# First attention of a two-layer kernel: each batch's normalisation, transpose and projection moved one period ahead, and its normalisation moved from VectorE to ScalarE

## The chip, the cores and the metric

The kernel runs on one core of one Trainium2 chip. The metric is the device time of one execution in microseconds (us). The engines are TensorE (PE, with its weight loads as PEld), VectorE (DVE), ScalarE (ACT), GpSimd (POOL) and SyncE (SP), which here only issues DMAs. Each engine works through its own list of instructions in order; they meet at semaphores alone.

## The reference, cut to what matters

The program computes two transformer layers. The change touches only the first attention of the first layer, whose input `x` has 16 batches of 256 tokens with 128 channels:

```python
h = _ln(x, ln1_g, ln1_b)                  # (x - mean) * rsqrt(var + 1e-5) * g + b
q, k, v = jnp.split(h @ w_qkv + b_qkv, 3, axis=-1)      # 16 heads of 8 channels
# buckets of 64 tokens; a bucket sees the one before it and, causally, itself
scores = where(mask, einsum('bnihd,bnjhd->bnhij', qb, kc) * scale, -inf)
ob = einsum('bnhij,bnjhd->bnihd', softmax(scores), vc)
x = x + ob @ w_out + b_out
h2 = _ln(x, ln2_g, ln2_b)                 # goes into the MLP and the first expert layer
```

What follows it (the dense MLP and eight dense experts, a second attention, a routed expert layer) is not changed.

## The kernel before, in words

`attention_0` runs from the start to 274 us of the span. It is a software pipeline over 16 batches, one batch (256 tokens, two tiles of 128 rows) entering in each period. Its order is written out by hand in `PARTS_0` (line 173): a period `s` has four parts, each a list of steps `(name, stage, k)`, and a step with stage `g` works in period `s` on batch `s - g`. `parts_0` (line 188) hands the same sequence to all engines, and each engine does what it has to do for a step (`step` under `block.gpsimd`, `scalar`, `vector`, `tensor`). So the place of a step in the list sets its place in four queues at once. "s3" below is the period with s = 3.

The front of a batch has these steps:

- `xstats`: VectorE takes mean and variance of two token tiles (lines 505 and 509).
- `power`: GpSimd turns variances into reciprocal roots (lines 369 and 370), in one pair of instructions for the first norm of batch `s` and the second norm of batch `s - 5`.
- `norm`: VectorE writes `hn = (x - mean) * rstd` (lines 525 and 527); GpSimd, in the same place, computes `shift2` (lines 390 and 392) for the second norm, and adds the output bias to `x` (line 403).
- `lift`: TensorE transposes `hn` (line 602) and, for the batch four behind, the attention output `ob` (line 606); ScalarE copies both out of PSUM as `hT` (line 429) and `aT` (line 431).
- `qk`: TensorE projects `hT` to keys and queries in fp32 (lines 610 and 611); ScalarE writes their fp16 high part (line 438), `low` on VectorE the rest (line 534). SyncE writes both to DRAM and reads them back in head order into one of three `kq` tiles (lines 337, 339 and 346), which the scores of the next period read.
- `vproj`: TensorE and VectorE make the values (lines 618 and 541).

In the period in which batch n has its scores (s = n + 2), part k has `scores` (PE lines 635 and 641, DVE row maxima line 547), `mpad` and `shift` (the maxima subtracted from the queries, line 562); `weights` one period later (PE line 657, ACT exp line 446, POOL causal mask line 411), `values` (PE line 670), `copy` and `back` (ACT line 451, PE line 679, DVE lines 570 and 571), `output` (PE line 693, DVE lines 580 and 582), `stats` (line 515), `norm2` (ACT line 457), PE transposes of `hn2` inside `output` (line 691), `halves2` (ACT lines 466 and 469, POOL line 395). `split` (ACT lines 474 and 476) and `wlow` (POOL line 398) prepare the dense weights of the next stage alongside.

Before, the front is split over the turn of a period: batch s has `xstats` in part 0, `power` in part 2 and `norm` in part 3 of period s; its `lift`, `qk` and `low` follow in part 0 of period s + 1, in front of the `weights` of that part. PSUM bank `WA` holds the transposes first and then the projection, so one batch's `lift` waits for the last `low`. Scores use two banks `S`, weights two banks `ST`.

SyncE also issues, behind the read-back of each batch, up to five DMAs that fill DRAM rows with a constant (`blanks`, line 356, 268 KB each, 72 in all), after batch 0 the rest of `x` and the dense constants and weights (lines 349, 2416 and 2423), and later further dense weights.

Of the kernel before, what the change touches and what calls it, by code (L numbers as in the profile page):

```python
# [9 lines left out]
P = 128  # L10
# [8 lines left out]
NC_ = T // CT  # L19
# [137 lines left out]
def unpacked(m, name):  # L157
# [4 lines left out]
    for part, shape in parts:  # L162
# [8 lines left out]


PARTS_0 = [
    [("scores", 2, 0), ("lift", 1, 0), ("vproj", 2, 0), ("shift", 3, 1), ("qk", 1, 0), ("xstats", 0, 0), ("low", 1, 0),
     ("weights", 3, 0), ("values", 4, 3), ("copy", 4, 1)],
    [("scores", 2, 1), ("mpad", 2, 0), ("output", 5, 0), ("back", 4, 1),
     ("weights", 3, 1), ("values", 3, 0), ("halves2", 6, 0), ("wlow", 0, 0)],
    [("scores", 2, 2), ("shift", 2, 0), ("stats", 0, 0),
     ("weights", 3, 2), ("power", 0, 0), ("values", 3, 1), ("copy", 3, 0)],
    [("scores", 2, 3), ("mpad", 2, 1), ("back", 3, 0), ("norm", 0, 0),  # L180
     ("weights", 3, 3), ("values", 3, 2), ("norm2", 5, 0), ("split", 0, 0)]]
STAGES_0 = 6
ONE_HIGH, ONE_LOW = 3, 19
AHEAD = NB - 2
# [3 lines left out]
def parts_0(step):  # L188

    for s in range(NB + STAGES_0 - 1):  # L190
        for part in PARTS_0:
            for what, stage, k in part:
                if what == "lift":
                    if s > 0:
                        step(what, s - 1, k)
                elif what in ("xstats", "stats", "power", "norm"):
                    if s < AHEAD + 5:
                        step(what, s, k)
                elif what in ("halves2", "norm2"):
                    if 0 <= s - stage < AHEAD:  # L200
                        step(what, s - stage, k)
                elif what == "split":
                    if 0 <= s - 2 < CUTS:
                        step(what, s - 2, k)
                elif what == "wlow":
                    if 0 <= s - 3 < CUTS:
                        step(what, s - 3, k)
                elif 0 <= s - stage < NB:
                    step(what, s - stage, k)


def attention_0(nc, d, keep, rows, heads, stages):
# [3 lines left out]
    with ExitStack() as ctx:  # L216
# [12 lines left out]
        mv = m.sb("mv", [P, 4, 2])  # L229
        half = m.sb("half", [P, 4])  # L230
        rstd = m.sb("rstd", [P, 4])
        shift2 = m.sb("shift2", [P, 2])
        hn2 = m.sb("hn2", [P, 2, C])
        h2 = m.sb("h2", [P, TB])
# [30 lines left out]
        xb_done = m.sem("xb_done")  # L265
        ln = m.sem("ln")
        var_done = m.sem("var_done")
        rstd_done = m.sem("rstd_done")
        pool_ln = m.sem("pool_ln")
        passed_pool, passed_dve = m.sem("passed_pool"), m.sem("passed_dve")  # L270
        hn_done = m.sem("hn_done")
        lift_full, lift_free = m.sem("lift_full"), m.sem("lift_free")
# [17 lines left out]
        x1_done = m.sem("x1_done")  # L290
        shift2_done, norm2_done = m.sem("shift2_done"), m.sem("norm2_done")
        h2_done, xh_done, xl_done = m.sem("h2_done"), m.sem("xh_done"), m.sem("xl_done")
        shift2_own = m.sem("shift2_own")
# [8 lines left out]
        def both_norms(n):  # L302
            return slice(0 if n < NB else 2, 4 if n >= 5 else 2)

        def toks2(n):
            return slice(n * TB, (n + 1) * TB)
# [13 lines left out]
        def _(sp):  # L320
# [6 lines left out]
                sp.wait_ge(kq_clear, p + 1)  # L327
                sp.dma_start(kq[p][ONE_HIGH:P:16, 0], d["unit"]).then_inc(ones_in, 16)
            sp.wait_ge(loaded, 16 * LOADS)
            sp.dma_start(x[:, 4:12, :], d["x"][:, 4:12, :]).then_inc(x_mid, 16)  # L330
            sp.dma_start(keep["gate0"][:], d["gate0"]).then_inc(gate_in, 16)
            for n in range(NB):
                planes = heads[n % 2]
                sp.wait_ge(high_done, n + 1)
                wait(sp, landed[n % 2], 48 * (n // 2))
                for i in (1, 3):
                    sp.dma_start(planes[i:i + 2].rearrange("s p t -> p s t"), high[:]).then_inc(high_out, 16)
                sp.wait_ge(low_done, n + 1)
                sp.dma_start(planes[0:6:5].rearrange("s p t -> p s t"), low[:]).then_inc(low_out, 16)

                sp.wait_ge(high_out, 32 * (n + 1))
                wait(sp, st_full, n * 8 - 16)
                for c, pair in enumerate((planes[2:4], planes[0:2], planes[4:6])):
                    if c == 1:
                        sp.wait_ge(low_out, 16 * (n + 1))
                    sp.dma_start(kq[n % 3][c:P:4, :, :, BK:BK + TB].rearrange("r s a t -> r (s a) t"),
                                 pair.rearrange("s (a r) t -> r (s a) t", a=4)).then_inc(landed[n % 2], 16)
                if n == 0:
                    sp.dma_start(x[:, 12:NT, :], d["x"][:, 12:NT, :]).then_inc(x_rest, 16)
                    keep["fetch_dense"](sp)  # L350
                    sp.wait_ge(blank_set, 1)
                if n % 2 == 0 and n >= 4:
                    sp.wait_ge(w_low, n - 2)
                    keep["fetch_set"](sp, n // 2)
                for i in range(5 * n, min(5 * n + 5, BLANKS * NC_)):
                    sp.dma_start(blanks[:, i], blank[:]).then_inc(blanked, 16)
            sp.wait_ge(w_low, 2 * E - 2)
            keep["fetch_set"](sp, E)
# [3 lines left out]
        def _(pool):  # L362
            def power(n):
                pool.wait_ge(var_done, n + 1)

                wait(pool, norm2_done, n - 5)
                settle(pool, passed_pool)
                t, v = Tally(pool, pool_ln, 1, n), both_norms(n)
                t.link(pool.tensor_scalar(rstd[:, v], mv[:, v, 1], EPS, 1.0, ALU.add, ALU.mult))
                pool.tensor_tensor(rstd[:, v], rstd[:, v], half[:, v], ALU.pow).then_inc(rstd_done, 1)  # L370

            pool.memset(half[:], -0.5).then_inc(half_set, 1)
            pool.wait_ge(half_set, 1)
# [8 lines left out]
            pool.wait_ge(loaded, 16 * LOADS)  # L382

            def step(what, n, k):
                if what == "power" and n:
                    power(n)
                if what == "norm" and n >= 5:

                    pool.wait_ge(rstd_done, n + 1)
# [6 lines left out]
                if what == "wlow":  # L396
                    pool.wait_ge(w_high, n + 1)
                    pool.tensor_tensor(cut_of(("w1l", "w2l"), n), stage[:, n // 2 % 2, n % 2],
                                       cut_of(("w1h", "w2h"), n), ALU.subtract).then_inc(w_low, 1)
                if what == "norm" and n < NB:  # L400
                    rows_landed(pool, n)
                    for a in range(2):
                        ins = pool.tensor_tensor(keep["xs"][:, 2 * n + a, :], x[:, 2 * n + a, :], bo[:], ALU.add)
                    ins.then_inc(xb_done, 1)
# [13 lines left out]
        def _(act):  # L418
# [6 lines left out]
            def step(what, n, k):  # L425
# [21 lines left out]
                if what == "copy":  # L447
                    act.wait_ge(pv_done, n * 8 + 4 * k + 4)

                    wait(act, back_full, n * 2 - 1 + k)  # L450
                    act.activation(ots[:, k, :], OT[:], ACT.Copy).then_inc(ot_free, 1)
                if what == "norm2":
                    act.wait_ge(shift2_done, n + 1)

# [28 lines left out]
        def _(dve):  # L483
            dve.memset(mpad[:], 0.0).then_inc(cleared, 1)
            for t in hT:
                dve.memset(t[:, 0:BK], 0.0).then_inc(cleared, 1)
            for t in kq[0:2]:
                dve.memset(t[:], 0.0).then_inc(kq_clear, 1)
            sums = Tally(dve, ln, 0, 0)

            def step(what, n, k):
# [9 lines left out]
                if what == "xstats" and n < NB:  # L501
                    wait(dve, rstd_done, n)
# [4 lines left out]
                    settle(dve, passed_dve)  # L507
                    for a in range(2):
                        ins = dve.bn_aggr(mv[:, a, :], st[:, a, :])
                        ins.then_inc(var_done, 1) if a and n < 5 else sums.inc(ins)  # L510
                if what == "stats" and n >= 5:
                    wait(dve, rstd_done, n)
# [4 lines left out]
                    settle(dve, passed_dve)  # L517
                    for a in range(2):
                        ins = dve.bn_aggr(mv[:, 2 + a, :], st[:, 2 + a, :])
                        ins.then_inc(var_done, 1) if a else sums.inc(ins)  # L520
                if what == "norm" and n < NB:

                    wait(dve, lift_full, n)
                    dve.wait_ge(rstd_done, n + 1)
                    dve.tensor_scalar(hn[:, 0, :], x[:, 2 * n, :], mv[:, 0, 0:1], rstd[:, 0:1],
                                      ALU.subtract, ALU.mult)
                    dve.tensor_scalar(hn[:, 1, :], x[:, 2 * n + 1, :], mv[:, 1, 0:1], rstd[:, 1:2],
                                      ALU.subtract, ALU.mult).then_inc(hn_done, 1)
                    if n == 0:
                        dve.memset(kq[2][:], 0.0).then_inc(kq_clear, 1)  # L530
# [2042 lines left out]
```

## Time and profile before

| | us |
|---|---|
| median of 3 runs | 1055.04 (1055.03 to 1056.13) |
| the profiled execution | 1056.1 |
| its span | 1054.3 |
| first attention within the span | 0 to 274 |
| PE busy over the span | 917.5 (87%) |
| DVE busy | 822.5 (78%) |
| ACT busy | 748.9 (71%) |
| POOL busy | 431.6 (41%) |

The span runs from the first to the last recorded instruction. Times of single rows are microseconds from its start. A row of the timeline gives start, duration, engine, line, operation, tiles, and how many like instructions it merges; in brackets stands the idle time of that engine just ahead of it and what ended it.

### The profile page before, as it was taken

To read this page: it belongs to the slowest core of one execution; us is meant where nothing else is said; L and a number is where in the kernel's file an instruction comes from. 1 tells how busy PE (TensorE), PEld (TensorE's weight loads), DVE (VectorE), ACT (ScalarE), POOL (GpSimd) and SP (SyncE) were. 2 spreads that over 40 slices of the span, in tenths; PEclk is the share of its full clock that TensorE was granted. 3 is DMA by queue.
4 is the path that set the end of the run, shared out by engine and by line. 5 is a ranking of instruction groups with operands and counts; after the bars stand their busy time and mean duration, and the time that the engine had idled before them with its cause. 6 is when DMAs were issued, how large, how long until landed. Compare 5 with 4: busy or idle time off the path is not lost. (4 is left out here: it accounts for less than half of the span.)

```text
span 1054.3 us, 28529 instructions
## 1 busy us (share of the span) xinstructions
PE 917.5 (87%) x9966; PEld 576.0 (55%) x9966; DVE 822.5 (78%) x2280; ACT 748.9 (71%) x1482; POOL 431.6 (41%) x613
## 2 busy tenths in 40 slices
PE   3688888887799999999999999869888865899995
PEld 2466656665355444444444444446556544788862
DVE  4587787875477799868899989958888867888854
ACT  1256666666799888888888878547677644688854
POOL 4255666667245200000000011014588877676653
PEclk9598999999799999999999999979999985999999
DMA  6635555541100000032122222111111102233318
GB/s 192 211 116 173 174 185 165 164 139 33 32 1 1 2 1 1 1 95 80 67 73 80 83 60 79 32 34 51 32 46 51 58 27 76 73 86 85 83 48 217
DMA packets 85578, 84.50 MB, mean 80 GB/s; under 512 B 8978, under 2 KB 62484, under 8 KB 85440
## 3 DMA queue, kind: packets, MB, share of 16 engines
q1 hardware_dynamic: 76240, 71.49, 22.0%
q0 software_dynamic: 4544, 8.60, 2.5%
q10 hardware_dynamic: 4656, 2.59, 0.9%
q8 instruction: 84, 1.38, 0.5%
q14 instruction: 54, 0.44, 0.1%
HBM read 45.77 MB, written 37.78 MB: 79 GB/s over the span
## 5 line engine op out<-in xcount | busy, mean ns | idle before, releaser
L931 ACT ACTIVATE d__hf<-keep__banks,dense__d 128x512 f32<-128x512 f32 x288 | 185.5, 680 | 48.2 <-PE keep__banks L1169 47.2
L995 DVE TENSOR_TENSOR d__hl<-d__hf,d__hh 128x1024 f16<-128x1024 f32 x144 | 174.1, 1220 | 28.0 <-ACT d__hh L936 25.8
L936 ACT ACTIVATE d__hh<-d__hf 128x1024 f16<-128x1024 f32 x144 | 152.2, 1057 | 4.6
L915 POOL TENSOR_SCALAR d__rstd<-d__mv 128x4 f32<-128x4 f32 x16 | 13.9, 869 | 336.7 <-DVE d__mv L1123 336.7
L411 POOL TENSOR_SCALAR_AFFINE_SELECT a__pt<-a__pt 128x512 f32<-128x512 f32 x128 | 81.5, 660 | 93.6 <-ACT a__pt L446 93.6
L1167 PE MATMUL keep__banks<-dense__xh,dense__w1h 128*128 128x512 f16 x288 | 109.9, 382 | 2.9 <-ACT d__hf L931 1.7
L1167 PE MATMUL keep__banks<-d__hh,dense__w2h 128*128 128x512 f16 x288 | 109.2, 379 | 2.4 <-DVE d__tmp L1052 2.4
L1169 PE MATMUL keep__banks<-dense__xh,dense__w1l 128*128 128x512 f16 x288 | 109.9, 381 | 0.0
L1168 PE MATMUL keep__banks<-dense__xl,dense__w1h 128*128 128x512 f16 x288 | 109.9, 381 | 0.0
L1168 PE MATMUL keep__banks<-d__hl,dense__w2h 128*128 128x512 f16 x288 | 109.2, 379 | 0.0
L1169 PE MATMUL keep__banks<-d__hh,dense__w2l 128*128 128x512 f16 x288 | 109.2, 379 | 0.0
L446 ACT ACTIVATE a__pt<-keep__banks 128x512 f32<-128x512 f32 x128 | 69.4, 596 | 43.7 <-PE keep__banks L657 43.6
L547 DVE TENSOR_REDUCE a__mx<-keep__banks 128x4 f32<-128x512 f32 x128 | 81.8, 682 | 20.4 <-PE keep__banks L641 20.2
L1458 POOL DMA_INDIRECT parts<-c__ys,c__dest x78 | 81.2, 1041 | 39.7 <-issue 16.6
L1897 POOL DMA_INDIRECT rows<-b__xr,b__slot x64 | 63.6, 994 | 21.5 <-issue 17.0
L1476 ACT ACTIVATE c__hf<-keep__banks,c__bias 128x256 f32<-128x256 f32 x156 | 61.1, 474 | 7.5 <-PE keep__banks L1685 6.4
L1697 PE MATMUL keep__banks<-routed__w2h,c__hh 128*128 x312 | 55.8, 219 | 5.4 <-DVE c__hl L1612 5.4
L1612 DVE TENSOR_TENSOR c__hl<-c__hf,c__hh 128x512 f16<-128x512 f32 x78 | 54.2, 695 | 2.7
L1699 PE MATMUL keep__banks<-routed__w2h,c__hl 128*128 x312 | 55.5, 219 | 0.0
L1698 PE MATMUL keep__banks<-routed__w2l,c__hh 128*128 x312 | 55.5, 219 | 0.0
L635 PE MATMUL keep__banks<-a__kq 32*64 32x128 f16 x1024 | 31.8, 229 | 20.7 <-DMA a__kq<-heads 18.3
L1167 PEld LDWEIGHTS keep__banks<-dense__xh,dense__w1h 128*128 128x128 f16 x288 | 30.4, 105 | 35.4 <-ACT d__hf L931 3.2
(353 smaller groups left out, 2330.8 us busy)
## 6 DMA issues: line engine op xcount, KB each, us to landing
rows<-a__blank SPq DMA_DIRECT2D x72, 268.0 KB, 3.8
d__G<-gates SPq DMA_DIRECT2D x64, 256.0 KB, 3.1
a__kq<-heads SPq DMA_DIRECT2D x48, 128.0 KB, 2.9
c__xin<-rows SPq DMA_DIRECT2D x39, 134.0 KB, 2.3
heads<-a__high SPq DMA_DIRECT2D x32, 128.0 KB, 2.2
dense__stage<-e_w SPq DMA_DIRECT2D x16, 256.0 KB, 3.6
b__stage<-e_w SPq DMA_DIRECT2D x32, 128.0 KB, 2.3
heads<-a__low SPq DMA_DIRECT2D x16, 128.0 KB, 2.0
```

Of the source, the lines that this page charges most:

```text
L411: pool.affine_select(out=v, in_=v, compare_op=ALU.is_ge, fill=0.0, base=BK, pattern=[[0, 8], [1, BK]], channel_multiplier=-1).then_inc(cau ...
L446: act.activation(pt[:, u % 4, :], ST[:, u % 2, :], ACT.Exp, scale=scale).then_inc(exp_done, 1)
L547: dve.tensor_reduce(mx[:, u // 4, :, u % 4], S[:, u % 2, :].rearrange("p (a j) -> p a j", a=4), AX.X, ALU.max).then_inc(s_free, 1)
L931: act.activation(hf[:, q, f], HB[:, f], gelu, scale=1.0 / WS, bias=b1[:, at:at + 1]).then_inc(s_["h_free"], 1)
L936: act.activation(hh[:, j % (LEAD + 1), f - 1:f + 1], hf[:, q, f - 1:f + 1], ACT.Copy).then_inc(s_["hi_done"], 1)
L995: dve.tensor_tensor(hl[:, p, f], hf[:, q, f], hh[:, p, f], ALU.subtract).then_inc(s_["lo%d_done" % i], 1)
L1167: pe.matmul(dst, wh, vh, start=begin, stop=False)
L1168: pe.matmul(dst, wh, vl, start=False, stop=False)
L1169: return pe.matmul(dst, wl, vh, start=False, stop=end)
L1458: pool.indirect_dma_start(parts, bass.IndirectOffsetOnAxis(dest[b % RING][:, a:a + 1], 0), ys[b % RING][:, a, :], None, bounds_check=2 * T ...
L1476: ins = act.activation(hf[b % 2][:, f], HB[:, b % 2, f // 2, f % 2], ACT.Gelu, scale=1.0 / WS, bias=bias[:, f, b:b + 1])
L1897: pool.indirect_dma_start(rows, bass.IndirectOffsetOnAxis(slot[n % SENT][:, k, a:a + 1], 0), words[n % SENT][:, a, :], None, bounds_check= ...
```

## The change

The steps of the front are regrouped. In period s, batch s now has `xstats` and a new `xpower` in part 0, a new step `hnorm` at the end of part 1, `lift` in part 2, `qk` and `low` in part 3. `hnorm` is two ScalarE activations (`Identity` with scale `rstd` and bias `shift`) in place of VectorE's two `tensor_scalar`. GpSimd computes that bias `shift = -mean * rstd` in `xpower`, so the power of the first norm and that of the second (`power2`) are now separate pairs. `norm2` moves from the end of part 3 to the front of the next part 0. `lift` of the attention output moves with `lift`. SyncE issues the second piece of `x` after batch 0 instead of ahead of it, the third piece, the dense data and the blanks after batch 1.

```diff
 PARTS_0 = [
-    [("scores", 2, 0), ("lift", 1, 0), ("vproj", 2, 0), ("shift", 3, 1), ("qk", 1, 0), ("xstats", 0, 0), ("low", 1, 0),
-     ("weights", 3, 0), ("values", 4, 3), ("copy", 4, 1)],
+    [("scores", 2, 0), ("norm2", 6, 0), ("vproj", 2, 0), ("shift", 3, 1), ("xstats", 0, 0),
+     ("weights", 3, 0), ("xpower", 0, 0), ("values", 4, 3), ("copy", 4, 1)],
     [("scores", 2, 1), ("mpad", 2, 0), ("output", 5, 0), ("back", 4, 1),
-     ("weights", 3, 1), ("values", 3, 0), ("halves2", 6, 0), ("wlow", 0, 0)],
-    [("scores", 2, 2), ("shift", 2, 0), ("stats", 0, 0),
+     ("weights", 3, 1), ("values", 3, 0), ("halves2", 6, 0), ("hnorm", 0, 0), ("wlow", 0, 0)],
+    [("norm", 0, 0), ("scores", 2, 2), ("lift", 0, 0), ("shift", 2, 0), ("stats", 0, 0),
      ("weights", 3, 2), ("power", 0, 0), ("values", 3, 1), ("copy", 3, 0)],
-    [("scores", 2, 3), ("mpad", 2, 1), ("back", 3, 0), ("norm", 0, 0),
-     ("weights", 3, 3), ("values", 3, 2), ("norm2", 5, 0), ("split", 0, 0)]]
+    [("scores", 2, 3), ("mpad", 2, 1), ("qk", 0, 0), ("back", 3, 0), ("low", 0, 0), ("sums", 0, 0),
+     ("weights", 3, 3), ("values", 3, 2), ("split", 0, 0)]]
@@ SyncE @@
             sp.wait_ge(loaded, 16 * LOADS)
-            sp.dma_start(x[:, 4:12, :], d["x"][:, 4:12, :]).then_inc(x_mid, 16)
-            sp.dma_start(keep["gate0"][:], d["gate0"]).then_inc(gate_in, 16)
             for n in range(NB):
...
                 if n == 0:
+                    sp.dma_start(x[:, 4:12, :], d["x"][:, 4:12, :]).then_inc(x_mid, 16)
+                    continue
+                if n == 1:
                     sp.dma_start(x[:, 12:NT, :], d["x"][:, 12:NT, :]).then_inc(x_rest, 16)
                     keep["fetch_dense"](sp)
+                    sp.dma_start(keep["gate0"][:], d["gate0"]).then_inc(gate_in, 16)
                     sp.wait_ge(blank_set, 1)
...
-                for i in range(5 * n, min(5 * n + 5, BLANKS * NC_)):
+                for i in range(5 * n - 5, min(5 * n, BLANKS * NC_)):
@@ GpSimd @@
             def power(n):
                 pool.wait_ge(var_done, n + 1)
-
-                wait(pool, norm2_done, n - 5)
+                wait(pool, hn_done, n)
                 settle(pool, passed_pool)
-                t, v = Tally(pool, pool_ln, 1, n), both_norms(n)
-                t.link(pool.tensor_scalar(rstd[:, v], mv[:, v, 1], EPS, 1.0, ALU.add, ALU.mult))
-                pool.tensor_tensor(rstd[:, v], rstd[:, v], half[:, v], ALU.pow).then_inc(rstd_done, 1)
+                t = Tally(pool, pool_ln, 1, n)
+                t.link(pool.tensor_scalar(rstd[:, 0:2], mv[:, 0:2, 1], EPS, 1.0, ALU.add, ALU.mult))
+                pool.tensor_tensor(rstd[:, 0:2], rstd[:, 0:2], half[:, 0:2], ALU.pow).then_inc(rstd_done, 1)
+                pool.tensor_scalar(shift[:], mv[:, 0:2, 0], -1.0, 1.0, ALU.mult, ALU.mult).then_inc(shift_own, 1)
+                pool.wait_ge(rstd_done, n + 1)
+                pool.wait_ge(shift_own, n + 1)
+                pool.tensor_tensor(shift[:], shift[:], rstd[:, 0:2], ALU.mult).then_inc(shift_done, 1)
+
+            def power2(n):
+                pool.wait_ge(var2_done, n + 1)
+
+                wait(pool, norm2_done, n)
+                settle(pool, passed_pool)
+                t = Tally(pool, pool_ln2, 1, n)
+                t.link(pool.tensor_scalar(rstd[:, 2:4], mv[:, 2:4, 1], EPS, 1.0, ALU.add, ALU.mult))
+                pool.tensor_tensor(rstd[:, 2:4], rstd[:, 2:4], half[:, 2:4], ALU.pow).then_inc(rstd2_done, 1)
@@ ScalarE @@
+                if what == "hnorm":
+
+                    wait(act, lift_full, n)
+                    act.wait_ge(shift_done, n + 1)
+                    for a in range(2):
+                        ins = act.activation(hn[:, a, :], x[:, 2 * n + a, :], ACT.Identity, scale=rstd[:, a:a + 1],
+                                             bias=shift[:, a:a + 1])
+                    ins.then_inc(hn_done, 1)
@@ VectorE @@
-                if what == "norm" and n < NB:
-
-                    wait(dve, lift_full, n)
-                    dve.wait_ge(rstd_done, n + 1)
-                    dve.tensor_scalar(hn[:, 0, :], x[:, 2 * n, :], mv[:, 0, 0:1], rstd[:, 0:1],
-                                      ALU.subtract, ALU.mult)
-                    dve.tensor_scalar(hn[:, 1, :], x[:, 2 * n + 1, :], mv[:, 1, 0:1], rstd[:, 1:2],
-                                      ALU.subtract, ALU.mult).then_inc(hn_done, 1)
...
```

The GpSimd step `sums` in part 3 keeps what `norm` did there (`shift2`, and the bias added to `x`); the wait of `xstats` on the last `rstd` becomes one on the last `shift`.

## Rows read from the trace of the kernel before

**Rows 1.** Timeline of PE: the scores that open s2, s3, s8, s16 and s17, and the first row of s18.
```profile
18.21 0.67 PE L635 MATMUL keep__banks<-a__kq 32*64 32x128 f16 x16 [7.24 <-DMA a__kq<-heads]
...
36.57 0.67 PE L635 MATMUL keep__banks<-a__kq 32*64 32x128 f16 x16 [7.34 <-DMA a__kq<-heads]
...
110.44 0.45 PE L635 MATMUL keep__banks<-a__kq 32*64 32x128 f16 x16 [0.62 <-DMA a__kq<-heads]
...
225.52 0.45 PE L635 MATMUL keep__banks<-a__kq 32*64 32x128 f16 x16
...
240.54 0.45 PE L635 MATMUL keep__banks<-a__kq 32*64 32x128 f16 x16 [0.50 <-DMA a__kq<-heads]
...
251.59 0.44 PE L606 MATMUL keep__banks<-keep__ident,a__ob 128*128 128x128 f32 x2
```

**Rows 2.** Busy time in period s11: length, PE, PEld, DVE, ACT, POOL, clock, DMA share, GB/s.
```profile
153.18:167.63 14.45, 12.06 (x311) 9.03 (x310) 11.47 (x33) 9.67 (x21) 9.27 (x17) 1.00 0.51 155
```

**Rows 3.** Timeline of PE in s11, from its lift on.
```profile
154.92 0.41 PE L602 MATMUL keep__banks<-keep__ident,a__hn 128*128 128x128 f32 x2 [0.97 <-DVE a__hn L527]
...
156.28 0.39 PE L647 MATMUL keep__banks<-a__a,a__mpad 128*128 128x128 f16 x4
157.50 0.70 PE L610 MATMUL keep__banks<-a__hT,a__a 128*128 128x256 f32 x2 [0.83 <-ACT a__aT L431]
...
158.57 0.41 PE L657 MATMUL keep__banks<-a__q,a__kq 32*128 32x64 f16 x16
...
159.49 0.45 PE L635 MATMUL keep__banks<-a__kq 32*64 32x128 f16 x16
...
160.09 0.38 PE L691 MATMUL keep__banks<-keep__ident,a__hn 128*128 128x128 f32 x2
...
161.02 0.66 PE L679 MATMUL keep__banks<-keep__ident,a__ots 128*128 128x128 f32 x4
161.61 0.40 PE L657 MATMUL keep__banks<-a__q,a__kq 32*128 32x64 f16 x16
...
163.51 0.38 PE L647 MATMUL keep__banks<-a__a,a__mpad 128*128 128x128 f16 x4 [0.21 <-DVE a__ob L571]
...
164.75 0.55 PE L635 MATMUL keep__banks<-a__kq 32*64 32x128 f16 x16
...
165.90 0.66 PE L679 MATMUL keep__banks<-keep__ident,a__ots 128*128 128x128 f32 x4 [0.27 <-ACT a__ots L451]
...
167.55 0.45 PE L635 MATMUL keep__banks<-a__kq 32*64 32x128 f16 x16
```

**Rows 4.** Timeline of DVE in s11: the normalisation of a batch.
```profile
154.18 0.34 DVE L525 TENSOR_SCALAR a__hn<-a__x,a__mv,a__rstd 128x128 f32<-128x128 f32 x1 [0.69 <-POOL a__rstd L370]
154.44 0.34 DVE L527 TENSOR_SCALAR a__hn<-a__x,a__mv,a__rstd 128x128 f32<-128x128 f32 x1
```

**Rows 5.** Timeline of POOL ahead of that normalisation.
```profile
151.42 1.27 POOL L411 TENSOR_SCALAR_AFFINE_SELECT a__pt<-a__pt 128x512 f32<-128x512 f32 x2
...
153.05 1.02 POOL L370 TENSOR_TENSOR a__rstd<-a__rstd,a__half 128x4 f32<-128x4 f32 x1
...
154.43 0.20 POOL L392 TENSOR_TENSOR a__shift<-a__shift,a__rstd 128x2 f32<-128x2 f32 x1
```

**Rows 6.** Timeline of ACT in s11.
```profile
154.66 0.88 ACT L457 ACTIVATE a__hn<-keep__lease,a__shift,a__rstd 128x128 f32<-128x128 f32 x2 [1.10 <-POOL a__shift L392]
...
162.05 1.08 ACT L446 ACTIVATE a__pt<-keep__banks 128x512 f32<-128x512 f32 x2 [1.08 <-PE keep__banks L657]
...
163.62 0.42 ACT L469 ACTIVATE dense__xh<-a__h 128x256 f16<-128x256 f32 x1
```

**Rows 7.** Timeline of SP: the writes of batches 0, 1 and 10, that start their round trips.
```profile
11.88 0.89 SPq L337 DMA_DIRECT2D heads<-a__high  x2
...
25.79 1.55 SPq L337 DMA_DIRECT2D heads<-a__high  x2
...
159.53 0.89 SPq L337 DMA_DIRECT2D heads<-a__high  x2
```

More of the change, by code:

```diff
@@ L193, in parts_0 @@
                 if what == "lift":
-                    if s > 0:
-                        step(what, s - 1, k)
-                elif what in ("xstats", "stats", "power", "norm"):
+                    if s < NB + 4:
+                        step(what, s, k)
+                elif what in ("stats", "power", "sums"):
                     if s < AHEAD + 5:
@@ L231, in attention_0 @@
         rstd = m.sb("rstd", [P, 4])
+        shift = m.sb("shift", [P, 2])
         shift2 = m.sb("shift2", [P, 2])
@@ L267, in attention_0 @@
         var_done = m.sem("var_done")
-        rstd_done = m.sem("rstd_done")
-        pool_ln = m.sem("pool_ln")
+        var2_done = m.sem("var2_done")
+        rstd_done, rstd2_done = m.sem("rstd_done"), m.sem("rstd2_done")
+        pool_ln, pool_ln2 = m.sem("pool_ln"), m.sem("pool_ln2")
         passed_pool, passed_dve = m.sem("passed_pool"), m.sem("passed_dve")
@@ L292, in attention_0 @@
         h2_done, xh_done, xl_done = m.sem("h2_done"), m.sem("xh_done"), m.sem("xl_done")
+        shift_own, shift_done = m.sem("shift_own"), m.sem("shift_done")
         shift2_own = m.sem("shift2_own")
@@ L300, in cut_of @@
             return keep[names[a]][:, e * CT:(e + 1) * CT]
-        def both_norms(n):
-            return slice(0 if n < NB else 2, 4 if n >= 5 else 2)
         def toks2(n):
@@ L384, in step @@
             def step(what, n, k):
-                if what == "power" and n:
+                if what == "xpower" and n:
                     power(n)
-                if what == "norm" and n >= 5:
-                    pool.wait_ge(rstd_done, n + 1)
+                if what == "power" and n >= 5:
+                    power2(n - 5)
+                if what == "sums" and n >= 5:
+                    pool.wait_ge(rstd2_done, n - 4)
                     pool.tensor_scalar(shift2[:], mv[:, 2:4, 0], -1.0, 1.0, ALU.mult, ALU.mult).then_inc(shift2_own, 1)
@@ L399, in step @@
                                        cut_of(("w1h", "w2h"), n), ALU.subtract).then_inc(w_low, 1)
-                if what == "norm" and n < NB:
+                if what == "sums" and n < NB:
                     rows_landed(pool, n)
@@ L486, in _ @@
                 dve.memset(t[:, 0:BK], 0.0).then_inc(cleared, 1)
-            for t in kq[0:2]:
-                dve.memset(t[:], 0.0).then_inc(kq_clear, 1)
+            dve.memset(kq[0][:], 0.0).then_inc(kq_clear, 1)
+            dve.memset(kq[1][:], 0.0).then_inc(kq_clear, 1)
             sums = Tally(dve, ln, 0, 0)
@@ L500, in step @@
                     dve.wait_ge(cleared, CLEARS)
-                if what == "xstats" and n < NB:
-                    wait(dve, rstd_done, n)
+                if what == "xstats":
+                    wait(dve, shift_done, n)
                     rows_landed(dve, n)
@@ L509, in step @@
                         ins = dve.bn_aggr(mv[:, a, :], st[:, a, :])
-                        ins.then_inc(var_done, 1) if a and n < 5 else sums.inc(ins)
+                        ins.then_inc(var_done, 1) if a else sums.inc(ins)
                 if what == "stats" and n >= 5:
-                    wait(dve, rstd_done, n)
                     wait(dve, shift2_done, n - 5)
@@ L519, in step @@
                         ins = dve.bn_aggr(mv[:, 2 + a, :], st[:, 2 + a, :])
-                        ins.then_inc(var_done, 1) if a else sums.inc(ins)
-                if what == "norm" and n < NB:
-                    wait(dve, lift_full, n)
-                    dve.wait_ge(rstd_done, n + 1)
-                    dve.tensor_scalar(hn[:, 0, :], x[:, 2 * n, :], mv[:, 0, 0:1], rstd[:, 0:1],
-                                      ALU.subtract, ALU.mult)
-                    dve.tensor_scalar(hn[:, 1, :], x[:, 2 * n + 1, :], mv[:, 1, 0:1], rstd[:, 1:2],
-                                      ALU.subtract, ALU.mult).then_inc(hn_done, 1)
-                    if n == 0:
-                        dve.memset(kq[2][:], 0.0).then_inc(kq_clear, 1)
+                        ins.then_inc(var2_done, 1) if a else sums.inc(ins)
+                if what == "norm" and n == 0:
+                    dve.memset(kq[2][:], 0.0).then_inc(kq_clear, 1)
                 if what == "low":
```

## The prediction

> **What bounds the kernel now.** I read the timeline of TensorE first, for the scores that open each period. The reader is to see three stretches [rows 1]: a start with two long waits for the read-back of keys and queries (7.24 and 7.34 us), a steady run from s8 to s16 of (225.52 - 110.44) / 8 = 14.39 us a period, and an end. Then the busy times in one steady period [rows 2]: of 14.45 us TensorE is busy 12.06, VectorE 11.47, ScalarE 9.67, GpSimd 9.27. No engine fills it, so a chain across engines sets it. The timelines name its members. TensorE waits 0.97 us ahead of the lift for VectorE's `hn` and 0.83 ahead of the projection for ScalarE's copy `aT` [rows 3]. VectorE's normalisation had itself waited 0.69 us for GpSimd's power [rows 4], which came behind a causal mask (1.27 us) in GpSimd's queue and took 1.02 us for four columns [rows 5]. The front of a batch is handed from engine to engine without work laid between the steps.
>
> **The change, part by part.** I walk one new steady period from lift to lift; where a step follows its forerunner directly I take the distance between starts in the old trace.
> - Part 2: the lift is followed by shift, weights, values and the scores of part 3. Lift and `vproj` together were 156.28 - 154.92 = 1.36 us; both stay on the path. Shift, weights and values to the next scores: 164.75 - 163.51 = 1.24.
> - Part 3: scores 160.09 - 159.49 = 0.60; projection 158.57 - 157.50 = 1.07; back transposes, weights, values to the next scores 167.55 - 165.90 = 1.65.
> - Part 0: scores 0.60, shift 0.39, then weights, values, the scores of part 1 and the output product 161.02 - 158.57 = 2.45.
> - Part 1: back transposes to the weights 161.61 - 161.02 = 0.59 [all rows 3]. From there the path leaves TensorE: weights, exps and `halves2` on ScalarE end at 163.62 + 0.42 = 164.04 [rows 6], 2.43 us after 161.61. Behind them stands the new `hnorm`, two activations of the kind of `norm2`: 0.88 us [rows 6]. To the lift 0.14, as from VectorE's end at 154.78 to 154.92 [rows 3, 4].
>
> Sum: 1.36 + 1.24 + 0.60 + 1.07 + 1.65 + 0.60 + 0.39 + 2.45 + 0.59 + 2.43 + 0.88 + 0.14 = 13.40 us, a gain of 1.0 per period. On TensorE itself the stretch from those weights to the lift is only about 0.34 + 0.58 + 0.60 = 1.5 us (weights, values, scores), so TensorE would still stand 3.45 - 1.5 = 1.9 us ahead of the lift. Both old waits go; this one is late next.
>
> Work that I cost at nothing, and its cover. GpSimd: one more power pair and one more shift pair; the pair on two columns in place of four is shorter, so I put the addition at 1.1 us, 10.4 in all, below the period. `xpower` follows the mask of part 0 and would give `shift` some 1 us ahead of `hnorm`; if that cover is gone, the lift is later by the excess, one for one. ScalarE: 0.88 more, 10.55 us. `norm2` now stands ahead of the exps of part 0; it fits while `split` ends 0.8 us before these weights do, and if not, the copy that the back transposes of part 1 need is late: by my walk it ends 0.1 to 0.2 us before TensorE comes to them, the thinnest cover of all. VectorE: 0.60 us less [rows 4], and no wait for power, since `xstats`, `stats` and `low` all read what was made parts ago. `low` waits for `high`, but the back step lies between, and scores and row maxima of the next part start together. SyncE: the same DMAs. Its new gate is the same wait on the weights of three batches before, which now end in the very part in which the write starts; they end first by a little. Queued behind it are read-back and blanks only.
>
> VectorE did a batch's normalisation in 0.60 us [rows 4], ScalarE needs 0.88 for the same shape [rows 6], and that stands on the path of every period. The Trainium skill, "ScalarE: Activation LUTs", section "Rules for kernel authors", speaks against it: multiplications and additions belong on VectorE. The rows agree as to the durations; by the rule the same order with VectorE normalising would gain 0.28 us more a period, some 3 us in all, if VectorE had it ready as early. What the rule leaves out is the place in the queue, worth the other 1.0.
>
> The **start**. Batch 0's front is longer by 0.28 us for ScalarE and some 0.4 for the two shift instructions, so its round trip starts at about 12.6 in place of 11.88 [rows 7]. Batch 1's front now waits for `low` of batch 0 (13.5), then takes statistics 0.9, `xpower` 1.5, `hnorm` 0.9, transposes and copy 1.3, projection 2.2 and high part 0.85, estimates at the durations of the first rows: write at about 21.3. Before, it was issued at 25.79 [rows 7], behind dense data and five blanks in SyncE's queue, and landed at 36.57 [rows 1]: 10.8 us, where batch 0's took 18.21 - 11.88 = 6.3. With those DMAs moved behind batch 1, I take 6.3: landed at 27.6. Then not the DMA but the work of s2 is last: it starts behind the projection of batch 1 at 20.1 and holds some 11.5 us, so s3 opens at 31.6 in place of 36.57: -5.0. The bounds are 36.57 + 0.7 (congestion as before) and 27.6.
> s3 to s7: 110.44 - 36.57 = 73.87 before. TensorE stood at its lower level in part of it (16 score matmuls took 0.67 us, later 0.45 [rows 1]). I take five periods of 13.5: -6.4. s8 to s15: 8 x 13.40 = 107.2 against 115.1: -7.9.
> s16: no front is left in it, since the last projection is now in s15. It took 240.54 - 225.52 = 15.0 and would take what s17 did without lift of `hn` and projection, 251.59 - 240.54 = 11.05: -4.0 [rows 1]. s17 and the end: nothing; the last value, back, lift and output steps are the same chain.
>
> Sum: -5.0 - 6.4 - 7.9 - 4.0 = -23.3, so 1056.1 - 23.3 = 1032.8 for the profiled execution. That execution was 1.1 us above the median, which makes 1031.7; some of the starts I used hold old waits (the 1.65 and 2.45 above), so I round down: **1031**.
>
> **The rivals.**
> 1. *The wait at the lift vanishes.* ScalarE's work up to `hnorm` comes earlier than I think, or TensorE is slower around it. Then VectorE is the bound: 11.47 - 0.60 busy and some 0.7 of hand-overs, 11.6 us a period. Eleven periods at 1.8 less: about 1011. For it: 11.47 is near. Against it: exps, `halves2` and `hnorm` have to follow the weights in ScalarE's queue, whatever TensorE does.
> 2. *ScalarE or GpSimd slips.* The copy in part 0 behind `norm2` and `split`, or the mask behind `xpower` and `power2`, makes TensorE wait as well: with 0.8 us more, 14.2 a period, eleven times, 1040. For it: both queues grow, to 10.5 us, and the cover is 0.2 us. Against it: each has 3 us of idle time in a period.
> 3. *Slower: the round trip becomes the bound.* The write of a batch starts 0.65 us before the next period and must be back one period later, so 13.4 + 0.65 = 14.05 us are there. A trip took 167.55 - 159.53 = 8.0 us or less in s11 [rows 3, 7], 10.8 behind blanks. It costs time above 14.05. To make the kernel slower it must also eat the gain elsewhere: at 17.5 us each of thirteen periods is 16.85, 3.4 more than mine, +44 in all, 1075; it breaks even near 15.9. Against it: blanks now follow a read-back by a whole period less its own length.
> 4. *No change.* Saved waits come back at one place per period, as `hn` late by 1.9 + 1.0 us and the start as congested as before: 1055.
>
> **How the numbers follow.** Forecast 0.64, rival 1 0.11, rival 2 0.17, rival 3 0.04, rival 4 0.04. The forecast's own range is 1024 to 1038: the start at its two bounds is -4 or +5, and the period uncertain by 0.3. With rival 2 whole, and reaching a third of the way to rival 1 for periods that fall between, the range is 1018 to 1044; left out are rivals 1, 3 and 4, 0.19. About 0.2%, 2 us, is what a measurement of this kernel can tell from no change. Faster by more: 0.64 + 0.11 + 0.17 = 0.92, and a little of rival 4; within it 0.04; slower 0.04.
>
> **What would show it.** In the changed trace: periods of 13.2 to 13.6 us between the opening scores from s7 to s16; TensorE idle 1.5 to 2 us ahead of the lift, ended by ScalarE's `hn`; no wait ahead of the projection; s3 opening near 31.6 and batch 1's write near 21.3; s16 of about 11. A period under 12, with no wait for `hn`, is rival 1. Waits of the back transposes for `ots`, or of values for the mask, with `hn` later than 2 us, are rival 2. Opening scores that wait for the read-back in steady periods are rival 3.

## The result, and the profile after

The changed kernel takes 1045.03 us (median of 6 runs, 1041.16 to 1047.99) against 1055.03 before (6 runs): ratio 0.9912, 95% interval 0.9883 to 0.9941. It is faster, by 10 us where 24 were forecast, and it stands outside the range of 1018 to 1044.

The page of the changed kernel. Its profiled execution took 1046.9 us:
```profile
span 1045.2 us, 28598 instructions
...
PE 925.2 (89%) x9966; PEld 588.5 (56%) x9966; DVE 810.5 (78%) x2248; ACT 761.4 (73%) x1514; POOL 445.1 (43%) x667
...
PEclk9698888988999999999999999969999965999998
```
VectorE lost 12 us of work, ScalarE and GpSimd gained 12.5 and 13.5, as planned. TensorE gained 7.7 us, though no matmul was added. The slices of PEclk are 26 us wide; the fourth to the tenth read 8 in all but one, where before they read 9 in all but one.

TensorE's timeline of the changed kernel, one row per question of the forecast (columns as in [rows 1]):
```profile
32.11 0.67 PE L650 MATMUL keep__banks<-a__kq 32*64 32x128 f16 x16
...
39.12 0.41 PE L672 MATMUL keep__banks<-a__q,a__kq 32*128 32x64 f16 x16 [3.16 <-ACT a__pt L462]
...
110.89 0.41 PE L617 MATMUL keep__banks<-keep__ident,a__hn 128*128 128x128 f32 x2 [1.65 <-ACT a__hn L473]
...
126.39 0.41 PE L617 MATMUL keep__banks<-keep__ident,a__hn 128*128 128x128 f32 x2 [1.65 <-ACT a__hn L473]
...
139.04 0.66 PE L617 MATMUL keep__banks<-keep__ident,a__hn 128*128 128x128 f32 x2 [1.65 <-ACT a__hn L473]
```
s3 opens at 32.11 (36.57 in [rows 1]). The two waits of [rows 3] are one now, 1.65 us ahead of the lift, and it is the same each time. The projection no longer waits. But the distances between lifts are not the same: 15.50 and 12.65 us here.

Windows from lift to lift (length; busy us and instructions of PE, PEld, DVE, ACT, POOL; granted clock; DMA share; GB/s), four periods in a row and then all of s8 to s15:
```profile
96.79:110.89 14.10, 12.45 (x303) 10.04 (x303) 10.97 (x31) 10.24 (x22) 10.26 (x21) 0.88 0.50 169
110.89:126.39 15.50, 13.85 (x303) 11.06 (x303) 10.95 (x31) 10.59 (x22) 10.29 (x21) 0.78 0.45 144
126.39:139.04 12.65, 11.01 (x302) 8.96 (x303) 10.71 (x31) 10.24 (x22) 10.28 (x21) 0.99 0.70 239
139.04:154.58 15.54, 13.89 (x302) 11.07 (x303) 11.10 (x32) 10.49 (x22) 10.36 (x21) 0.79 0.42 124
...
102.90:218.11 115.21, 101.44 (x2423) 81.34 (x2417) 87.32 (x249) 83.22 (x177) 82.32 (x160) 0.87 0.52 171
```
Every period holds the same some 303 matmuls, and the same busy time of VectorE, ScalarE and GpSimd. What differs is TensorE's clock. At a granted clock of 0.99 the period is 12.65 us, shorter than the forecast of 13.40; at 0.88 it is 14.10, at 0.78 it is 15.50. In each of the four, TensorE's busy time and the 1.65 us add up to the period: it waits at the lift and nowhere else. Before, the clock was 1.00 in a steady period [rows 2].

Three windows of one microsecond around one lift show where it falls:
```profile
137.04:138.04 1.00, 0.36 (x5) 0.08 (x2) 0.94 (x4) 0.97 (x4) 1.00 (x3) 1.00 0.95 327
138.04:139.04 1.00, 0.00 (x0) 0.03 (x1) 1.00 (x2) 0.86 (x3) 1.00 (x2) 0.84 0.97 356
139.04:140.04 1.00, 0.99 (x6) 0.94 (x7) 0.14 (x1) 0.00 (x0) 1.00 (x2) 0.50 0.99 354
```
TensorE runs nothing from 137.39 to 139.04 (the last row ahead of the lift starts at 137.00 and takes 0.39 us). Within that wait the granted clock drops from 1.00 to 0.50, and the work of the next period starts at 1.2 GHz in place of 2.4. That is why the lift's row at 139.04 holds two transposes in 0.66 us instead of 0.41. Most falls come a little later, with TensorE already at work again, which is why the lift at 110.89 still took 0.41. Behind the lift at 82.63, windows from it on:
```profile
82.63:83.63 1.00, 1.00 (x24) 0.88 (x24) 0.11 (x1) 0.34 (x1) 1.00 (x2) 1.00 0.98 347
83.63:84.63 1.00, 1.00 (x54) 0.78 (x49) 0.85 (x5) 1.00 (x4) 0.27 (x1) 0.74 1.02 367
84.63:85.63 1.00, 1.00 (x19) 0.77 (x17) 0.21 (x3) 0.96 (x2) 0.84 (x2) 0.50 0.37 133
```
Ten lifts, from 82.63 to 210.49 us, wait 1.65 us. The clock fell at seven of them and not at the other three (126.39, 184.22 and 197.25).

The gain and the loss, in us of the span:

| stretch | before | after | change | forecast |
|---|---|---|---|---|
| start to s3 | 36.57 | 32.11 | -4.5 | -5.0 |
| s3 to s7 | 73.87 | 70.79 | -3.1 | -6.4 |
| s8 to s15 | 115.08 | 115.21 | +0.1 | -7.9 |
| s16 | 15.02 | 11.32 | -3.7 | -4.0 |
| s17 to the first dense matmul | 33.31 | 32.11 | -1.2 | 0 |
| the rest, unchanged code | 780.45 | 783.66 | +3.2 | 0 |

Eight steady periods, the core of the change, brought nothing.

### The profile page after: what moved, and what is told of

Same layout as the page of the kernel before. It is cut to its first block and busy times, and to the rows that moved or that the text cites. A ratio compares the mean times of both kernels' runs of the same rounds, so it can differ in the third digit from the quotient of the medians.

```text
span 1045.2 us, 28598 instructions
## 1 busy us (share of the span) xinstructions
PE 925.2 (89%) x9966; PEld 588.5 (56%) x9966; DVE 810.5 (78%) x2248; ACT 761.4 (73%) x1514; POOL 445.1 (43%) x667
## 5 line engine op out<-in xcount | busy, mean ns | idle before, releaser
L685 PE MATMUL keep__banks<-a__pt,a__va 128*32 128x64 f32 x2048 | 48.6, 238 | 3.2 <-POOL a__pt L427 2.3
```

## The experiments

Two theories stood at the start. **A, the clock:** the chain got shorter as forecast, but the waits of TensorE are now one long one per period, in which its clock falls; the lost time is TensorE working at half speed after it. **B, the chain:** the added work of ScalarE or GpSimd stretches some periods (the second rival of the forecast), and TensorE's clock falls because it has to wait. Diffs are against the changed kernel unless it says otherwise. A ratio is to the kernel before as it ran beside that variant on the same chip, with its 95% interval in brackets; the variants ran on three chips, where the kernel before had medians of 1053.2 to 1054.4 us, so a difference of one or two us between medians from different chips says nothing. The windows given are from the values' projection (`vproj`) of s8 to that of s16; for the changed kernel that is
```profile
103.51:218.72 115.21, 101.44 (x2419) 81.34 (x2417) 87.31 (x248) 83.22 (x177) 82.32 (x161) 0.87 0.53 172
```
The kernel before held 95.35 us of TensorE work in 115.77 there, at a clock of 1.00.

### Work in the wait

Six transposes that nobody reads, on TensorE ahead of its wait for `hn`:
```diff
+                        if n >= 5:
+                            for _ in range(6):
+                                pe.transpose(WA[:, 0:P], ident[:], ident[:])
                         pe.wait_ge(hn_done, n + 1)
```


> The changed kernel with six transposes of the identity (1.3 us of TensorE work, overwritten by the lift) in each period from s5 on, in the place where TensorE stands 1.65 us waiting for hn. They make nothing earlier. Theory A (the wait lets TensorE's clock fall, and the low clock ate the gain): no low stretch between about 75 and 225 us, periods of 12.7 to 13.2 us in place of 14.1 and 15.5, first attention some 10 us shorter, 1034 to 1036 in all. Theory B (the long periods come from a chain across engines, and the clock records are a by-product): periods of 14.1 and 15.5 stay or grow where the filler runs over, 1045 or more.

Measured: 1033.9 us (1029.13 to 1034.75), ratio 0.9792 [0.9740, 0.9845], 11 us less than the changed kernel. The lift in TensorE's timeline, and the window:
```profile
94.06 0.82 PE L617 MATMUL keep__banks<-keep__ident 128*128 128x128 f32 x6
...
95.79 0.44 PE L620 MATMUL keep__banks<-keep__ident,a__hn 128*128 128x128 f32 x2 [0.90 <-ACT a__hn L473]
```
```profile
102.52:206.72 104.20, 94.37 (x2466) 77.74 (x2465) 86.75 (x248) 81.26 (x175) 80.86 (x158) 1.00 0.57 186
```
The six took 0.82 us and not the 1.3 expected. The filler cuts the wait to 0.90 us; the lift comes no earlier than ScalarE allows. Added work that nobody uses took 11 us off these eight periods, and the clock is 1.00. B has no place for that. The same filler in the kernel before is the control:

> The kernel before with the filler of the first experiment (six transposes of the identity ahead of the lift, in a wait of 1 us). Its clock stays at the full level from 100 to 260 us anyway. Theory A (the filler helps only by keeping the clock): no gain, 1054 to 1057 where it overruns the wait. Theory C (the filler helps by something else, such as an earlier issue of what follows): a gain here too, 1045.

Measured: 1053.09 us (1049.80 to 1056.97), ratio 0.9993 [0.9973, 1.0012]; no effect, where the clock had stood at 1.00 anyway. So the filler is worth something only where the long wait is.

### A shorter wait, a longer wait

`hnorm` ahead of `halves2` in part 1, so that ScalarE gives `hn` 1 us earlier:
```diff
-     ("weights", 3, 1), ("values", 3, 0), ("halves2", 6, 0), ("hnorm", 0, 0), ("wlow", 0, 0)],
+     ("weights", 3, 1), ("values", 3, 0), ("hnorm", 0, 0), ("halves2", 6, 0), ("wlow", 0, 0)],
```


> The changed kernel with hnorm ahead of halves2 on ScalarE in part 1. Theory A: hn comes 0.95 us earlier, the wait at the lift falls from 1.65 to about 0.7 us, the period to about 12.2 at the full level, and the low stretches become few or none: 1025 to 1030. Theory B: the period falls by at most 0.95 us everywhere and the low stretches stay: 1036.

Measured: 1031.3 us (1027.88 to 1033.58), ratio 0.9767 [0.9719, 0.9816]. The wait at the lift is 0.72 to 1.06 us, once 1.34. From `vproj` to `vproj` the periods at full level are 11.85 to 13.5 us. In two of the eight the clock fell all the same. The second fall came 1 us behind the lift that waits 1.34 us (at 200.07), the first within a wait of another kind:
```profile
107.44 0.41 PE L617 MATMUL keep__banks<-keep__ident,a__hn 128*128 128x128 f32 x2 [0.72 <-ACT a__hn L473]
...
124.04 0.64 PE L685 MATMUL keep__banks<-a__pt,a__va 128*32 128x64 f32 x13 [2.19 <-issue]
```
```profile
121.85:124.04 2.19, 0.00 (x1) 0.00 (x0) 0.31 (x3) 0.84 (x2) 2.19 (x3) 0.68 1.03 383
...
100.07:206.80 106.73, 94.04 (x2418) 75.26 (x2417) 87.89 (x249) 82.87 (x177) 83.72 (x164) 0.95 0.57 186
```
That period took 16.8 us. "issue" means that nothing the profile shows held TensorE up.

The other way, two more ScalarE copies of `x` into a scrap tile ahead of `hnorm`:
```diff
+                    if n >= 5:
+                        for a in range(2):
+                            act.activation(hx[:, a, :], x[:, 2 * n + a, :], ACT.Copy)
```


> The changed kernel with two more activations of the same size on ScalarE ahead of hnorm from s5 on (0.8 us, result unused). Theory A: the wait at the lift is 2.5 us, and low stretches come in every period: periods of 15.5 to 17, some 1065. Theory B: each of eleven periods is 0.8 us longer, 1054.

Measured: 1050.7 us (1048.37 to 1056.12, 10 runs), ratio 0.9977 [0.9952, 1.0003]. The lift in TensorE's timeline, and the window:
```profile
140.98 0.66 PE L621 MATMUL keep__banks<-keep__ident,a__hn 128*128 128x128 f32 x2 [2.05 <-ACT a__hn L477]
```
```profile
105.69:221.69 116.00, 99.63 (x2418) 80.51 (x2417) 86.87 (x248) 86.12 (x193) 81.69 (x161) 0.88 0.52 170
```
The two copies took 0.49 us together and not 0.8, so the wait grew by 0.4 us. Theory A as I had put it expected more low stretches and was wrong in that: the clock is 0.88, against 0.87 in the changed kernel, and periods are 13.0, 14.5 and 16.0 us, each some 0.4 longer. Here 0.4 us more of wait cost its own length and no more of the clock.

### VectorE normalises, in the new place

ScalarE's two activations of `hnorm` are taken out, and VectorE does the same step in the same place of the list:
```diff
+                if what == "hnorm":
+                    wait(dve, lift_full, n)
+                    dve.wait_ge(rstd_done, n + 1)
+                    dve.tensor_scalar(hn[:, 0, :], x[:, 2 * n, :], mv[:, 0, 0:1], rstd[:, 0:1],
+                                      ALU.subtract, ALU.mult)
...
```


> The changed kernel with VectorE writing hn at the end of its part 1, in place of ScalarE's two activations; the order of all other steps stays. hn should be done some 0.5 us earlier (VectorE ends its back step at 6.75 us of the period and needs 0.60). Theory A: wait at the lift about 1.1 us, period 12.4 at the full level, fewer low stretches, 1030 to 1038. Theory B: 1040. If VectorE becomes the bound, its row maxima of part 2 start 0.6 us later and the period stays at 13.

Measured: 1038.44 us (1035.27 to 1039.48), ratio 0.9841 [0.9792, 0.9890]. The wait falls to 1.25 to 1.40 us at five of the eight lifts in the window (0.79, 1.74 and 1.89 at the others), and the clock comes part of the way back (lift, then window):
```profile
137.15 0.41 PE L616 MATMUL keep__banks<-keep__ident,a__hn 128*128 128x128 f32 x2 [1.40 <-DVE a__hn L543]
```
```profile
98.73:208.56 109.83, 94.80 (x2418) 76.12 (x2417) 94.11 (x265) 76.84 (x161) 82.85 (x163) 0.94 0.56 182
```
The clock fell twice in the window: at 122.9 us, within an "issue" wait of 1.37 us that follows the lift with 1.74, and behind the lift that waits 1.27 (at 173.99). It did not fall at the lift that waits 1.89. The interval of the ratio just touches that of the changed kernel (0.9883 to 0.9941), but the slowest of the four executions, 1039.48 us, is shorter than the fastest of sixteen of the changed kernel, 1039.92. So of the two halves of the change, the new order is what pays; the move to ScalarE costs time, some 6 us by the medians.

### SyncE's order alone, and all but that

The kernel before with only the new order of DMAs:

> The kernel before with SyncE's new order alone: second piece of x after batch 0, the rest, dense data and blanks after batch 1. The write of batch 1 should be issued at about 23.6 us in place of 25.8 and its read-back land near 30, so s3 opens at 31 to 32 in place of 36.6. My account of the start gives that reordering nearly all of the 4.5 us that the changed kernel gained there: about 1050. Rival: the congestion moves to batch 2 and the gain is given back in s4: 1054.

Measured: 1056.02 us (10 runs), ratio 1.0025 [1.0006, 1.0043]: no gain, and the rival held, that it is given back in s4. ScalarE's and TensorE's rows of this kernel show the gain come and go:
```profile
32.00 0.67 PE L637 MATMUL keep__banks<-a__kq 32*64 32x128 f16 x16 [2.19 <-DMA a__kq<-heads]
```
```profile
37.97 0.63 ACT L476 ACTIVATE dense__stage<-dense__stage 128x512 f32<-128x512 f32 x1 [13.53 <-DMA dense__stage<-m_w]
```
```profile
39.76 1.22 PE L612 MATMUL keep__banks<-a__hT,a__a 128*128 128x256 f32 x2 [4.00 <-ACT a__hT L431]
```
s3 opens at 32.00, 4.6 us earlier, as in the changed kernel. Then ScalarE stands in its queue for dense weights whose fetch was moved behind batch 1, the copy `hT` comes late behind it, and s4 begins where it did before (its `vproj` at 53.65, before 53.64).

The other half, the changed kernel with SyncE's old order, ran beside the changed kernel itself on one chip:

> The changed kernel itself, run beside the next two on one chip. Theory A: again low stretches of the clock between 80 and 225 us and a wait of 1.65 us at the lift; 1042 to 1048. Rival (the low stretches belonged to one chip or one execution): few of them, 1033.

> The changed kernel with SyncE's old order: dense data and blanks again ahead of batch 1. Alone on the old kernel the new order gave nothing. If its worth is only in the new front, batch 1's read-back is again last here: s3 opens at about 36 and the kernel takes 1048 to 1050. If the start is given back in s3 whatever the order, 1045.

Measured: 1047.51 us (ratio 0.9939 [0.9905, 0.9973]) for the changed kernel, 1049.16 (0.9965 [0.9945, 0.9986]) with the old order, 10 runs each. The intervals overlap. The old order opens s3 at 36.25 but reaches s8 at 103.53 against 104.71, so whether the new order of DMAs is worth anything in whole stays open. The profile of the first shows the same pattern in another execution of the changed kernel, on another chip: from 83.82 us on the wait is 1.65 at nine of ten lifts (1.46 at the tenth), the clock fell at seven of the ten, and the periods from `vproj` to `vproj` are some 12.5, 14.1 and 15.6 us.

### The lift later, and the fetch earlier

If the wait is the fault, the lift should stand where `hn` is ready. Here it moves behind the weights of part 2:
```diff
-    [("norm", 0, 0), ("scores", 2, 2), ("lift", 0, 0), ("shift", 2, 0), ("stats", 0, 0),
-     ("weights", 3, 2), ("power", 0, 0), ("values", 3, 1), ("copy", 3, 0)],
+    [("norm", 0, 0), ("scores", 2, 2), ("shift", 2, 0), ("stats", 0, 0),
+     ("weights", 3, 2), ("lift", 0, 0), ("power", 0, 0), ("values", 3, 1), ("copy", 3, 0)],
```


> The changed kernel with the lift behind shift and weights of part 2 in place of ahead of them: TensorE has 0.7 us of work in front of hn. Theory A: wait about 0.9 us, few low stretches, but ScalarE's copies of the lift now follow the exps, so the projection may wait for them some 0.5 us: periods of 12.3 to 12.8, about 1032. Theory B: as the changed kernel, 1045.

Measured: 1027.55 us (1025.21 to 1028.12), ratio 0.9749 [0.9722, 0.9776]. The lift, and the window:
```profile
93.16 0.41 PE L617 MATMUL keep__banks<-keep__ident,a__hn 128*128 128x128 f32 x2 [0.49 <-ACT a__hn L473]
```
```profile
97.84:197.43 99.59, 90.36 (x2418) 71.88 (x2417) 85.99 (x249) 81.77 (x177) 81.95 (x161) 1.00 0.61 199
```
12.45 us a period, with 11 us less TensorE time for the same 2418 matmuls than the changed kernel. Both moves together:

> Both edits: hnorm ahead of halves2, lift behind the weights of part 2. hn is ready when TensorE comes to the lift; VectorE is then the bound at 11.6 to 12.0 us a period. Theory A: clock at the full level, about 1024 to 1028. Theory B: 1035 or more.

Measured: 1028.67 us (ratio 0.9765 [0.9736, 0.9794]), no better than the late lift alone. The periods did not come down to the 12.0 expected: most are 12.3 to 12.5 us, and one, in which the clock fell behind an "issue" wait of 1.00 us, is 14.6. The wait at the lift is gone in nearly all periods, and the projection waits instead:
```profile
170.35 0.70 PE L625 MATMUL keep__banks<-a__hT,a__a 128*128 128x256 f32 x2 [0.45 <-ACT a__aT L447]
```

Last, the late lift with the first set of dense weights fetched before batch 1, directly behind the second piece of `x`:
```diff
                     sp.dma_start(x[:, 4:12, :], d["x"][:, 4:12, :]).then_inc(x_mid, 16)
+                    keep["fetch_set"](sp, 0)
                     continue
...
-                for j in range(2):
-                    fetch_set(sp, j)
+                fetch_set(sp, 1)
```


> The late lift, and the first dense weights (two DMAs of 256 KB) fetched behind the second piece of x, ahead of batch 1's write, so that ScalarE's first split no longer waits 3.6 us for them with the exps of s3 behind it. TensorE's 3.2 us wait in s3 should go and s4 open some 3 us earlier: 1024 to 1026. Rival: batch 1's round trip becomes longer by more than its 4 us of slack, and nothing is gained: 1027.5.

Measured: 1022.57 us (1021.43 to 1025.00), ratio 0.9705 [0.9665, 0.9744], the lowest median of all and 25 us below the changed kernel beside it on the same chip. ScalarE no longer waits for the weights:
```profile
32.26 0.63 ACT L499 ACTIVATE dense__stage<-dense__stage 128x512 f32<-128x512 f32 x1
```
`vproj` of s4 starts at 46.12 in place of 49.53 with the late lift alone: 3.4 us. Whether the whole kernel is faster than with the late lift alone is less sure: the intervals of the two ratios overlap, and the profiled executions have the same span, 1023.3 and 1023.5 us. In this one 2.4 us go again between s8 and s16 (102.01 against 99.59), where the clock fell once:
```profile
152.79:153.79 1.00, 0.75 (x20) 0.49 (x20) 1.00 (x3) 1.00 (x4) 1.00 (x3) 1.00 1.01 371
153.79:154.79 1.00, 0.93 (x4) 0.66 (x4) 0.85 (x5) 0.89 (x2) 1.00 (x2) 0.58 1.02 364
```
No long wait precedes that fall. The nearest ones are 0.58 us for VectorE, up to 152.79, and 0.32 ahead of the lift at 153.86.

## Why the prediction was wrong

**The step that failed** is "s8 to s15: 8 x 13.40 = 107.2 against 115.1: -7.9", and in it the durations of TensorE from [rows 3], which were taken at the clock of 1.00 that [rows 2] show and carried into a period with another pattern of waits. The walk itself held, with some us to spare. From the weights of part 1 to the lift it had 2.43 + 0.88 + 0.14 = 3.45 us. ScalarE's timeline of the changed kernel (the exps and what follows them to `hn`):
```profile
123.49 1.08 ACT L462 ACTIVATE a__pt<-keep__banks 128x512 f32<-128x512 f32 x2 [1.17 <-PE keep__banks L672]
124.46 0.57 ACT L490 ACTIVATE a__h<-keep__banks,dense__d 128x256 f32<-128x256 f32 x1
125.06 0.42 ACT L493 ACTIVATE dense__xh<-a__h 128x256 f16<-128x256 f32 x1
125.38 0.86 ACT L473 ACTIVATE a__hn<-a__x,a__shift,a__rstd 128x128 f32<-128x128 f32 x2
```
The weights had started at 123.05 and the lift at 126.39: 3.34. From lift to weights it had 13.40 - 3.45 = 9.95; in the period at full level that stretch took 135.71 - 126.39 = 9.32, in the one before, with the same work, 123.05 - 110.89 = 12.16. The 2.8 us between the two are clock. Even the wait was forecast, 1.9 us against 1.65; what it does to the clock was not among the costs or the rivals. The filler run shows it: with the wait filled, the eight periods take 104.2 us, less than the 107.2 forecast. So the term had two errors. The clock, put at nothing, cost 11 us (115.2 - 104.2); the walk, 13.40 a period where 13.0 were measured at full clock, was 3 us too long over the eight and hid a part of it.

The trace of the kernel before already had a warning, outside the rows that I took. In s6 TensorE stood still for 1.03 us, and its clock fell there too:
```profile
93.78 0.40 PE L657 MATMUL keep__banks<-a__q,a__kq 32*128 32x64 f16 x8 [1.03 <-issue]
```
```profile
92.78:93.78 1.00, 0.00 (x0) 0.00 (x0) 0.93 (x4) 0.00 (x0) 0.83 (x3) 0.91 0.79 280
93.78:94.78 1.00, 1.00 (x36) 0.91 (x40) 0.56 (x3) 0.57 (x2) 0.89 (x2) 0.50 0.99 354
```

**The second miss** is "five periods of 13.5: -6.4" for s3 to s7, which came to -3.1. One part is again the clock (the lifts at 82.63 and 96.79 wait 1.65 us too, and their periods are 14.16 and 14.10 us). The other is a DMA that I moved without asking who waits for it. TensorE waits 3.16 us in s3, and ScalarE's and SyncE's rows of the changed kernel say why:
```profile
36.72 0.63 ACT L498 ACTIVATE dense__stage<-dense__stage 128x512 f32<-128x512 f32 x1 [3.66 <-DMA dense__stage<-m_w]
37.91 1.06 ACT L462 ACTIVATE a__pt<-keep__banks 128x512 f32<-128x512 f32 x2
```
```profile
21.85 0.88 SPq L335 DMA_DIRECT2D heads<-a__high  x2
...
30.05 0.91 SPq L2438 DMA_DIRECT2D dense__stage<-m_w  x2
```
The dense weights are issued at 30.05, and the exps stand behind their split in ScalarE's queue. The last run of the section before takes that wait away and gains 3.4 us in s3. The two parts together are more than the 3.3 us missed, because the periods between them were shorter than the 13.5 forecast: 12.08 and 12.34 us from `vproj` to `vproj` of s4 to s6.

**What was right.** Batch 1's write started at 21.85 (21.3 forecast), s3 opened at 32.11 (31.6), s16 took 11.3 (11.05), the projection does not wait, and the busy times of the engines came as summed. GpSimd's and ScalarE's longer queues did no harm (rival 2): in the steady periods shown they are busy the same 10.2 to 10.6 us, short or long, and TensorE waits for neither the masks nor the copies. s17 and the end, put at nothing, gave 1.2 us; their cause is not known. Rival 1, VectorE as the bound at 11.6 us a period, is not reached in any run: the shortest, eight periods of the late lift, average 12.45. The read-back (rival 3) is not waited for in steady periods.

**VectorE or ScalarE.** VectorE needs 0.60 us for a normalisation where ScalarE needs 0.88 [rows 4, 6]. The Trainium skill, "ScalarE: Activation LUTs", section "Rules for kernel authors", would leave multiplications and additions to VectorE. I had put that at 3 us; the run with VectorE in the new place is 6.6 us faster than the changed kernel, since a shorter wait also spares the clock: TensorE's work in the window fell from 101.44 to 94.80 us. The trace agrees with the rule, and by more than the durations alone say.

**What stays open.** The rest of the span, whose code is the same, took 783.66 us against 780.45; in the profiles of the other runs it lay between 780.3 and 785.1, so I take it as scatter of the execution, without proof. Why the clock falls at seven of ten equal waits and not at the other three stays open too. Whether the new order of DMAs is worth anything by itself is not settled either. Nor is what holds TensorE in an "issue" wait.

## What to carry to other kernels

When a change gathers several short waits of TensorE into one longer one, its price need not be the sum of the waits: look at the granted clock behind the waits that the trace already has before forecasting with durations taken at full clock, and put a price on its fall. The cure that paid most here was to place the waiting step later in the list, where its input is ready; work laid in the gap did it too. And of every DMA that is moved back in a queue, name the instruction that waits for it, and what stands behind that one.

## What the runs showed of the hardware

- In the changed kernel a wait of 1.65 us once per period was followed by a fall of TensorE's granted clock from 1.00 to 0.50, 2.4 to 1.2 GHz, at seven of ten lifts. Those periods were 1.5 or 2.9 us longer than the 12.65 us of one at full level. The fall came within the wait (139.04) or up to 1.5 us behind it, with TensorE already at work (82.63).
- The shorter the waits at the lift, the higher the mean clock from s8 to s16, by and large: 0.88 with 2.05 us, 0.87 and 0.88 with 1.65 (two executions), 0.94 with mostly 1.25 to 1.40, 0.95 with mostly 0.72 to 1.06, 1.00 with 0.90 beside the filler, 1.00 with 0.15 to 0.55 (late lift); 0.98 in each of the last two runs, whose waits at the lift are no longer than those but which had one fall each. Before, with 0.97 and 0.83 us in one period [rows 3], it was 1.00.
- The length of a single wait does not settle it. In the run with VectorE a lift that waits 1.89 us had no fall behind it and one that waits 1.27 us had; the last run had a fall with no wait over 0.6 us in the 10 us ahead of it.
- TensorE shows "issue" waits of up to 2.19 us in some periods of the faster kernels, and one of 1.03 us in the kernel before. In the filler run:
```profile
101.93 0.43 PE L653 MATMUL keep__banks<-a__kq 32*64 32x128 f16 x12 [1.08 <-issue]
```
The load of the DMA engines does not explain them. The wait of 2.19 us in the run with `hnorm` first came at a DMA share of 1.03, one of 1.43 us in the run with VectorE at a share of 0.04:
```profile
216.06:217.49 1.43, 0.00 (x1) 0.00 (x0) 0.70 (x5) 0.77 (x2) 1.43 (x2) 1.00 0.04 10
```
What they are stays open.
